# A decoder layer on one core: where the gate product y, the sums of x and attention's setup stand

## The chip, the cores and the metric

The kernel runs on one core of a Trainium2 chip. A core has five engines with a queue of instructions each: TensorE (PE in the profile; PEld is its weight load), VectorE (DVE), ScalarE (ACT), GpSimd (POOL) and SyncE (SP), which here only starts transfers. They wait for one another by semaphores. The metric is the time of one execution in microseconds, from the device; less is better.

## What is computed

One decoder layer over 16 sequences of 256 tokens with 256 features, each part followed by a residual sum and a LayerNorm:

```python
def _L0_attn_ref(x, ...):                    # the mixer
    xh, gate = split(x @ W_in.T + b_in)
    xh = silu(causal_conv(xh, conv_w) + conv_b)
    s  = scan of (xh @ W_ssm.T + b_ssm)      # one number for each token
    y  = (s * xh + Dv * xh) * silu(gate)
    return y @ W_out.T + b_out + x
def _L0_xattn_ref(query, key, value, ...):   # 16 heads of 16, key = value = ctx
    return softmax(q @ k.T / 4) @ v @ Wo.T + bo
def _L0_ffn_ref(x, Wr, W1, W2):              # router, 8 experts of capacity 640
    ...
x = _layernorm(x + _L0_attn_ref(x, ...))
x = _layernorm(x + _L0_xattn_ref(x, ctx, ctx, ...))
x = _layernorm(x + _L0_ffn_ref(x, ...))
```

## The kernel before

Three functions run one after the other, each a block with one program for each engine. `mixer_in` (to about 143 us) makes `gated`, the product of `xh` and silu of the gate, for all tokens, and the scan's result, which four transfers write to HBM. `attend` (to about 680 us) does the rest of the mixer, the cross attention and the router, and sends the rows to their experts. `experts` does the experts and the last LayerNorm.

`attend` is a software pipeline over the 16 sequences, here called batches. A step `n` has 16 slots `h`, and every engine's program walks the same slots, doing for each what its list says. In step n, batch n+1 is in its first stage (lag −1: `y`, output projection of the mixer, residual `r`, LayerNorm), batch n makes k and q, batch n−1 takes row maxima of the scores, batches n−2 and n−3 the exponentials and weighted sums, and batch n−4 the router and the scatter. A step from 6 to 13 is run by a loop of two; the others are written out. What the order is in a queue is what is written: an engine never passes a waiting instruction. TensorE alone loads weights ahead.

The places that matter here, by line:

- L1032, VectorE, slot 7: `y = (sb + d_col) * gated` in four chunks of 128 × 256, one semaphore count `y_done` after the fourth. Both tensors are in SBUF. `sb` is the scan's row, broadcast by a transfer (L521).
- L707, TensorE, slots 11 and 13: `mixer_out`, the product of `y` with the output weights, two halves of tokens; each sums over the four chunks. The first half waits for `y_done`.
- L984, VectorE, and L744, TensorE, even slots: the scores of two heads go to PSUM and VectorE takes their row maxima `nmax`. TensorE's scores of the next even slot wait for the maxima of this one, since there is one buffer.
- L615 and L617, GpSimd, `residual`: `x2b = x + b_out`, then `x2b + x`, both 128 × 512. VectorE's `r` (L1062, slot 13) adds `x2b` to the product and waits for `x_added`.
- L621, GpSimd, `split_lo`: the low half of k, and of q, for a product in two halves. Its input is ScalarE's cast (L876). SyncE then writes both to HBM and reads them back in another layout.
- L650, GpSimd: two indirect transfers that scatter a batch's rows to their experts; they wait for `dest` (L1048, VectorE, slot 10).
- L1039 to L1056, VectorE, slots 8 to 11: `place`, `carry`, `over`, `slot`, and `onrm`, which TensorE waits for.
- L602 to L606, L949 to L958: attention's setup. GpSimd fills 32 rows in each half of `kst` with ones, of which row 48 of each half is used (the others are overwritten by keys or unused). VectorE scales the weights and bias of q (`w_q_sb`, `bq`) and casts `tri` and `ones`.

GpSimd's order in a step is what this quotes (L621, L615, L650 are the calls' contents):

```python
if on(n, 0): split_lo(n, s["k_hi"], s["k_split"])
if on(n, 4): ...                     # norm of batch n - 4, L633 to L639
if on(n, 0) and on(n, -1): residual(n + 1, q)
if on(n, 0): split_lo(n, s["q_hi"], s["q_split"])
if on(n, 4): ...                     # the scatter, L645 to L653
```

## Time and profile before

| | us |
|---|---|
| median of 3 runs | 957.1 (956.09 to 959.01) |
| the profiled execution | 958.14 |
| its span, first to last instruction | 956.4 |
| mean granted TensorE clock | 0.927 |
| busy: PE, PEld, DVE, ACT, POOL | 802.6, 638.8, 611.7, 401.8, 357.6 |

The profile covers one execution. A busy time is the time in which an engine has an instruction in work; the share of a whole span mixes stages with different limits. The releaser of a wait is inferred from semaphores: it names what came last. Rows of a timeline merge instructions that follow one another, so that the duration is that from the first one's start to the last one's end.

### The profile page before, as it was taken

Reading aid. Unit: us, or ns where it says so; the run is one execution under the profiler, and the core shown is the slowest. Engines: PE = TensorE matmul, PEld = TensorE weight load, DVE = VectorE, ACT = ScalarE, POOL = GpSimd, SP = SyncE. Lnnn points to the kernel's source line nnn. Section 1 sums busy time; section 2 is a strip of 40 time slices with the busy share of each in tenths; the row PEclk is TensorE's granted clock in tenths of the full one; section 3 lists DMA queues with packets and bytes.
Section 4 is the critical chain, followed back from the end, with each engine's and each line's share of the span. In section 5 each row is a group of like instructions: output and inputs, shape, how many; then the busy total and the mean of one; then the engine's idle time right before and its main releaser. Section 6 shows DMA issues by size and latency. Waiting matters only on the chain. (4 is left out here: it accounts for less than half of the span.)

```text
span 956.4 us, 16891 instructions
## 1 busy us (share of the span) xinstructions
PE 802.6 (84%) x5933; PEld 638.8 (67%) x5933; DVE 611.7 (64%) x1410; ACT 401.8 (42%) x639; POOL 357.6 (37%) x290
## 2 busy tenths in 40 slices
PE   5999864678988889988889898874599999999992
PEld 3777653455766666666666675542499999999982
DVE  4888847365787887787887877533245555545542
ACT  4665631135544545444555456540334233423320
POOL 0333326322345454344544343233122254325422
PEclk9999887689999999999999999885599999999997
DMA  4115501645435534435434434102432333234000
GB/s 123 45 46 168 169 2 53 156 138 139 135 120 151 149 116 114 148 118 158 124 116 135 133 114 143 45 31 85 131 102 74 117 126 100 76 115 140 22 27 18
DMA packets 75913, 100.91 MB, mean 106 GB/s; under 512 B 10961, under 2 KB 63354, under 8 KB 75856
## 3 DMA queue, kind: packets, MB, share of 16 engines
q1 hardware_dynamic: 72400, 92.03, 32.3%
q0 software_dynamic: 3456, 8.13, 2.4%
q8 instruction: 34, 0.56, 0.2%
q14 instruction: 23, 0.19, 0.1%
HBM read 65.47 MB, written 35.74 MB: 106 GB/s over the span
## 5 line engine op out<-in xcount | busy, mean ns | idle before, releaser
L984 DVE TENSOR_REDUCE nmax<-ps_m 128x4 f32<-128x1024 f32 x128 | 156.4, 1222 | 56.4 <-PE ps_m L744 49.2
L938 ACT ACTIVATE pt<-ps_a 128x1024 f32<-128x1024 f32 x128 | 131.3, 1026 | 120.2 <-PE ps_a L754 87.4
L1249 ACT ACTIVATE hid<-ps_h 128x640 fp32r<-128x640 f32 x64 | 45.1, 705 | 152.1 <-PE ps_h L1189 152.1
L1189 PE MATMUL ps_h<-xt,w_hi 128*128 128x320 f32 x512 | 100.7, 319 | 1.0 <-DVE xt L1264 1.0
L744 PE MATMUL ps_m<-kst,qst 48*128 48x256 f32 x512 | 67.6, 344 | 34.1 <-DVE nmax L984 28.7
L1298 DVE SCALAR_TENSOR_TENSOR hid<-ps_h,hid 128x640 fp32r<-128x640 f32 x64 | 52.8, 825 | 57.0 <-ACT hid L1249 56.5
L744 PEld LDWEIGHTS ps_m<-kst,qst 48*128 48x128 f32 x512 | 40.5, 195 | 72.0 <-DVE nmax L984 47.5
L1201 PE MATMUL ps_y<-w_hi,hid 128*128 128x256 f32 x640 | 85.3, 284 | 1.7 <-issue 1.7
L1189 PEld LDWEIGHTS ps_h<-xt,w_hi 128*128 128x128 f32 x512 | 80.6, 192 | 5.5 <-DVE hid L1298 3.6
L1201 PEld LDWEIGHTS ps_y<-w_hi,hid 128*128 128x128 f32 x640 | 80.1, 191 | 1.9 <-issue 1.9
L707 PE MATMUL ps_d<-w_out_sb,y 128*128 128x256 f32 x256 | 67.3, 412 | 11.2 <-DVE y L1032 10.9
L166 POOL TENSOR_TENSOR gated<-xh,sgate 128x512 f32<-128x512 f32 x32 | 42.3, 1321 | 90.1 <-ACT xh L259 90.1
L354 DVE SCALAR_TENSOR_TENSOR conv<-ps_xh,taps,conv 128x510 f32<-128x510 f32 (+2 forms) x96 | 71.7, 747 | 3.4
L769 PE MATMUL ps_o<-pt,vals 128*32 128x256 f32 x1024 | 71.3, 398 | 0.0
L1345 POOL DMA_INDIRECT out_rows<-gated,token x40 | 39.4, 986 | 84.1 <-issue 84.1
L621 POOL TENSOR_TENSOR half<-kq,half 128x512 fp32r<-128x512 f32 x32 | 42.7, 1335 | 71.8 <-ACT half L876 71.8
L650 POOL DMA_INDIRECT rows_dram<-pay,dest x32 | 33.1, 1035 | 86.0 <-DVE dest L1048 76.0
L707 PEld LDWEIGHTS ps_d<-w_out_sb,y 128*128 128x128 f32 x256 | 50.3, 206 | 19.8 <-issue 11.5
L1312 DVE SCALAR_TENSOR_TENSOR gated<-ps_y,gated 128x256 f32<-128x256 f32 x40 | 19.3, 483 | 64.8 <-PE ps_y L1201 61.6
L1189 PE MATMUL ps_h<-xt,w_lo 128*128 128x320 f32 x256 | 59.1, 312 | 0.0
L1333 POOL TENSOR_TENSOR w_lo<-gated,w_hi 128x2048 fp32r<-128x2048 f32 x8 | 47.4, 5919 | 28.0 <-ACT w_hi L1239 27.9
L754 PE MATMUL ps_a<-qst,kst 49*128 49x256 f32 x512 | 53.9, 289 | 0.8 <-ACT pt L938 0.5
(169 smaller groups left out, 1623.8 us busy)
## 6 DMA issues: line engine op xcount, KB each, us to landing
halves_dram<-half SPq DMA_DIRECT2D x64, 256.0 KB, 2.6
gated<-in_w SPq DMA_DIRECT2D x16, 1024.0 KB, 5.2
kst<-halves_dram SPq DMA_DIRECT2D x64, 128.0 KB, 2.6
qst<-halves_dram SPq DMA_DIRECT2D x64, 128.0 KB, 2.9
rows_dram<-blank SPq DMA_DIRECT2D x1, 5160.0 KB, 19.4
gated<-rows_dram SPq DMA_DIRECT2D x8, 645.0 KB, 4.2
x_raw<-in_x_t SPq DMA_DIRECT2D x8, 512.0 KB, 3.8
xres<-in_x SPq DMA_DIRECT2D x16, 256.0 KB, 4.1
```

The source lines that it names most:

```text
L354: op = nc.vector.scalar_tensor_tensor(out[:, :, late:S], ps[:, :, 0:S - late], taps[:, m, k:k + 1], out[:, :, late:S], ALU.mult, ALU.add)
L707: mm = pe.matmul(ps_d[:, t * D:(t + 1) * D], y[:, m, t * P:(t + 1) * P], w["out"][:, m, :], start=(m == 0), stop=(m == MH - 1), skip_group ...
L744: mm = pe.matmul(ps_m[:, side, t, :], qst[base:base + MR, p, k, t * P:(t + 1) * P], kst[base:base + MR, p, k, :], start=True, stop=True, s ...
L754: mm = pe.matmul(ps_a[:, side, t, :], kst[base:base + MR + 1, p, k, t * P:(t + 1) * P], qst[base:base + MR + 1, p, k, :], start=True, stop ...
L769: mm = pe.matmul(ps_o[VW * i:VW * (i + 1), g, :], vals[:, p, t, h, :], pt[:, h // 2 % 4, h % 2, t, :], start=(t == 0), stop=(t == KT - 1), ...
L938: nc.scalar.activation(pt[:, k % 4].rearrange("p s t q -> p (s t q)"), ps_a[:].rearrange("p s t q -> p (s t q)"), ACT.Exp).then_inc(s["exp ...
L984: nc.vector.tensor_reduce(nmax[:, q, :, :, h // 2].rearrange("p t s -> p s t"), ps_m[:], AX.X, ALU.max, negate=True).then_inc(s["max_done" ...
L1189: mm = pe.matmul(ps_h[:, f % 2, c2, 0:HC], w1[a][:, p, k, f * P:(f + 1) * P], xt[:, b, p, k, c2 * HC:(c2 + 1) * HC], start=(n == 0 and k = ...
L1201: mm = pe.matmul(ps_y[:, (p + t) % 2, 0:D], hid[:, a, f, t * P:(t + 1) * P], w2[b][:, p, f, :], start=(n == 0 and f == 0), stop=(n == 2 an ...
L1249: nc.scalar.activation(hid[:, HI, f, :].rearrange("p (c n) -> p c n", c=2), ps_h[:, f % 2, :, 0:HC], ACT.Relu).then_inc(s["hid_hi"], 1)
L1298: nc.vector.scalar_tensor_tensor(hid[:, LO, f, :].rearrange("p (c n) -> p c n", c=2), ps_h[:, f % 2, :, 0:HC], 0.0, hid[:, HI, f, :].rearr ...
L1333: nc.gpsimd.tensor_tensor(flat(w2[LO][:, p]), flat(w2_raw), flat(w2[HI][:, p]).bitcast(F32), ALU.subtract).then_inc(s["w2_lo"], 1)
```

## The change

`y` goes from slot 7 to slot 9 on VectorE, behind the maxima of slot 8 and the first `onrm`, and counts `y_done` after each of the four chunks; the first half of `mixer_out` waits chunk by chunk. On GpSimd the sums of x go behind the subtraction for q and behind the scatter. The scaled weights and bias and the casts are made by ScalarE at the end of `mixer_in`'s program, in tiles that outlive it. The memsets of `kst` are gone: ScalarE copies the ones into a tile of 32 × 128, and SyncE copies that by two transfers into the one row of `kst` per half that is read. The waits on the setup change with it.

```diff
@@ mixer_in, ScalarE @@
             xh_of(MH * NG - 1)
             inject_out(NG - 1)
+            act.wait_ge(c["loaded"], 16 * len(c["loads"]))
+            nc.scalar.mul(c["w"]["q"][:], c["w"]["q"][:], HD ** -0.5).then_inc(c["scaled"], 1)
+            nc.scalar.mul(c["bq"][:], c["b_q"][:], HD ** -0.5).then_inc(c["scaled"], 1)
+            nc.scalar.copy(c["tri_b"][:], c["tri"][:]).then_inc(c["scaled"], 1)
+            nc.scalar.copy(c["ones_b"][:], c["ones"][:]).then_inc(c["scaled"], 1)
+            nc.scalar.copy(c["ones_r"][:], c["ones"][0:NH * S // P, :]).then_inc(c["scaled"], 1)
@@ attend, SyncE @@
-                need(sp, s["y_done"], j - 1)
+                need(sp, s["y_done"], MH * (j - 1))
...
-                sp.wait_ge(s["setup_pool"], 3)
+                settled(sp)
...
+            for base in SIDES:
+                sp.dma_start(kst[base + MR:base + MR + 1, :, :, :].rearrange("o b k t -> o (b k t)").bitcast(F32),
+                             c["ones_r"][:].bitcast(F32)).then_inc(s["ones_in"], 16)
             sp.wait_ge(c["scan_out"], 64)
@@ attend, GpSimd @@
-            for base in SIDES:
-                nc.gpsimd.memset(kst[base + 2 * HD:base + 4 * HD, :, :, :].bitcast(F32), 1.0).then_inc(s["setup_pool"], 1)
-            pool.wait_ge(s["setup_pool"], 3)
...
-                if on(n, 0) and on(n, -1):
-                    residual(n + 1, q)
                 if on(n, 0):
                     split_lo(n, s["q_hi"], s["q_split"])
...
                         ).then_inc(sent[p], 16)
+                if on(n, 0) and on(n, -1):
+                    residual(n + 1, q)
@@ attend, TensorE @@
-            pe.wait_ge(s["setup_dve"], 6)
-            pe.wait_ge(s["setup_pool"], 3)
+            pe.wait_ge(s["setup_dve"], 2)
+            pe.wait_ge(c["scaled"], 5)
+            pe.wait_ge(s["ones_in"], 32)
...
-                    pe.wait_ge(s["y_done"], j + 1)
...
                 for m in range(MH):
+                    if t == 0:
+                        pe.wait_ge(s["y_done"], MH * j + m + 1)
@@ attend, VectorE @@
-            nc.vector.tensor_scalar(w["q"][:], w["q"][:], SCALE, None, ALU.mult).then_inc(s["setup_dve"], 1)
-            nc.vector.tensor_scalar(bq[:], c["b_q"][:], SCALE, None, ALU.mult).then_inc(s["setup_dve"], 1)
-            nc.vector.tensor_copy(tri[:], c["tri"][:]).then_inc(s["setup_dve"], 1)
-            nc.vector.tensor_copy(ones_b[:], ones[:]).then_inc(s["setup_dve"], 1)
...
-                    if h == 7 and on(n, -1):
+                    if h == 9 and on(n, -1):
                         dve.wait_ge(s_in[q], use(n + 1, 16, q))
                         need(dve, s["wout_mm"], n + 1)
                         for m in range(MH):
-                            op = nc.vector.scalar_tensor_tensor(y[:, m, :], sb[:, q], c["d_col"][:, m:m + 1],
-                                                                gated[:, m, bass.ds((n + 1) * S, S)], ALU.add, ALU.mult)
-                        op.then_inc(s["y_done"], 1)
+                            nc.vector.scalar_tensor_tensor(y[:, m, :], sb[:, q], c["d_col"][:, m:m + 1],
+                                                           gated[:, m, bass.ds((n + 1) * S, S)], ALU.add, ALU.mult
+                                                           ).then_inc(s["y_done"], 1)
```

VectorE in the loop of `attend`, slots 7 to 10, before (`L984` are the maxima, `L1032` is `y`, `L1048` is `dest`):

```order
L1027 TENSOR_TENSOR carry<-carry,hot 128x8
...
L1032 SCALAR_TENSOR_TENSOR y<-sb,d_col_sb,gated 128x256
...
L984 TENSOR_REDUCE nmax<-ps_m 128x2x2
L1037 TENSOR_REDUCE place<-sel 128x2
L1039 TENSOR_TENSOR carry<-carry,hot 128x8
L1042 TENSOR_SCALAR over<-place 128x2
...
L1056 TENSOR_TENSOR onrm<-ps_e,rec 128x256
...
L984 TENSOR_REDUCE nmax<-ps_m 128x2x2
L1048 TENSOR_TENSOR dest<-slot,over 128x2
```

And with the change:

```order
L1027 TENSOR_TENSOR carry<-carry,hot 128x8
...
L984 TENSOR_REDUCE nmax<-ps_m 128x2x2
L1030 TENSOR_REDUCE place<-sel 128x2
L1032 TENSOR_TENSOR carry<-carry,hot 128x8
L1035 TENSOR_SCALAR over<-place 128x2
...
L1049 TENSOR_TENSOR onrm<-ps_e,rec 128x256
...
L1056 SCALAR_TENSOR_TENSOR y<-sb,d_col_sb,gated 128x256
...
L984 TENSOR_REDUCE nmax<-ps_m 128x2x2
L1041 TENSOR_TENSOR dest<-slot,over 128x2
```

The four instructions of `y` moved over one pair of maxima and six small operations, and stand directly ahead of the maxima of slot 10 and `dest`.

GpSimd in the same loop, before:

```order
L637 TENSOR_SCALAR twice<-pay,mv,ve 128x256 x2
...
L615 TENSOR_TENSOR x2b<-xres,b_out_sb 128x512
...
L617 TENSOR_TENSOR x2b<-x2b,xres 128x512
L621 TENSOR_TENSOR half<-kq,half 128x512
L650 DMA rows_dram<-pay,dest 5120x258 x2
L656 TENSOR_TENSOR ve<-ve,power 128x2
```

And with the change:

```order
L639 TENSOR_SCALAR twice<-pay,mv,ve 128x256 x2
L623 TENSOR_TENSOR half<-kq,half 128x512
L650 DMA rows_dram<-pay,dest 5120x258 x2
...
L617 TENSOR_TENSOR x2b<-xres,b_out_sb 128x512
...
L619 TENSOR_TENSOR x2b<-x2b,xres 128x512
L658 TENSOR_TENSOR ve<-ve,power 128x2
```

The two sums moved from ahead of the subtraction for q to behind the scatter's two transfers, which wait for `dest`.

## Rows read from the trace of the kernel before

**Rows 1.** Busy time by stretch: PE, PEld, DVE, ACT, POOL, granted clock, DMA share, GB/s
```profile
363.00:393.00 30.00, 26.53 (x213) 19.01 (x213) 23.12 (x57) 14.73 (x26) 13.27 (x12) 0.94 0.45 130
393.00:421.00 28.00, 24.87 (x213) 17.92 (x213) 23.17 (x57) 14.75 (x26) 13.28 (x12) 1.00 0.40 123
```
**Rows 2.** Timeline, batch 10 in step 9: start, duration, engine, line, operation, idle before
```profile
407.86 0.51 PE L744 MATMUL ps_m<-kst,qst 48*128 48x256 f32 x4 [0.48 <-DVE nmax L984]
...
408.61 0.61 ACT L876 CAST half<-kq 128x512 fp32r<-128x512 f32 x1
408.74 3.70 DVE L1032 SCALAR_TENSOR_TENSOR y<-sb,d_col_sb,gated 128x256 f32<-128x256 f32 x4
408.87 1.48 POOL L617 TENSOR_TENSOR x2b<-x2b,xres 128x512 f32<-128x512 f32 x1
...
410.31 1.45 POOL L621 TENSOR_TENSOR half<-kq,half 128x512 fp32r<-128x512 f32 x1
...
412.36 1.22 DVE L984 TENSOR_REDUCE nmax<-ps_m 128x4 f32<-128x1024 f32 x1
...
413.63 0.50 PE L744 MATMUL ps_m<-kst,qst 48*128 48x256 f32 x4 [1.71 <-DVE nmax L984]
...
414.18 0.42 DVE L1056 TENSOR_TENSOR onrm<-ps_e,rec 128x256 f32<-128x256 f32 x1
...
415.65 0.15 DVE L1048 TENSOR_TENSOR dest<-slot,over 128x2 int32<-128x2 f32 x1
...
416.66 1.09 POOL L650 DMA_INDIRECT rows_dram<-pay,dest  x1 [4.90 <-DVE dest L1048]
...
418.07 0.97 POOL L650 DMA_INDIRECT rows_dram<-pay,dest  x1 [0.31 <-issue]
...
421.07 0.69 DVE L1062 TENSOR_TENSOR r<-ps_d,x2b 128x512 f32<-128x512 f32 x1 [2.32 <-PE ps_d L707]
```
**Rows 3.** Timeline, step 15, which has no `y` and no sums of x
```profile
581.31 1.30 POOL L621 TENSOR_TENSOR half<-kq,half 128x512 fp32r<-128x512 f32 x1 [2.04 <-ACT half L876]
...
581.44 1.20 DVE L1042 TENSOR_SCALAR over<-place 128x2 f32<-128x2 f32 x1
```
**Rows 4.** Timeline, attention's start, and the landing times of the loads of `sb`
```profile
143.30 7.23 POOL L606 MEMSET kst<- 32x4096 f32 x2
...
144.86 0.36 SPq L521 DMA_DIRECT2D sb<-scan_dram  x1
...
150.61 1.26 POOL L615 TENSOR_TENSOR x2b<-xres,b_out_sb 128x512 f32<-128x512 f32 x1
...
151.22 3.13 DVE L1032 SCALAR_TENSOR_TENSOR y<-sb,d_col_sb,gated 128x256 f32<-128x256 f32 x4 [0.20 <-DVE b_o_sb L958]
...
154.50 5.08 PE L707 MATMUL ps_d<-w_out_sb,y 128*128 128x256 f32 x16 [9.72 <-DVE y L1032]
...
162.51 0.84 ACT L867 ACTIVATE kq<-ps_d,b_k_sb 128x256 f32<-128x256 f32 x2 [27.93 <-PE ps_d L687]
...
DMA to landing us min/median/max: 3.0/3.7/4.1
```
**Rows 5.** Timeline, step 1, in which batch 2 has its `y`
```profile
191.70 1.23 DVE L984 TENSOR_REDUCE nmax<-ps_m 128x4 f32<-128x1024 f32 x1 [1.56 <-PE ps_m L744]
...
192.61 1.27 POOL L621 TENSOR_TENSOR half<-kq,half 128x512 fp32r<-128x512 f32 x1 [4.84 <-ACT half L876]
...
196.54 0.50 PE L744 MATMUL ps_m<-kst,qst 48*128 48x256 f32 x4
...
201.60 2.03 PE L687 MATMUL ps_d<-ctx,w_k_sb 128*128 128x256 f32 x4 [2.19 <-DMA ctx<-in_ctx_t]
```
**Rows 6.** Timeline, step 14, in which batch 15 has its `y`
```profile
554.22 1.66 DVE L1032 SCALAR_TENSOR_TENSOR y<-sb,d_col_sb,gated 128x256 f32<-128x256 f32 x4
...
559.49 0.15 DVE L1048 TENSOR_TENSOR dest<-slot,over 128x2 int32<-128x2 f32 x1
...
564.88 0.69 DVE L1062 TENSOR_TENSOR r<-ps_d,x2b 128x512 f32<-128x512 f32 x1 [2.32 <-PE ps_d L707]
```

More of the change, by code:

```diff
@@ L400, in attend @@
     gated = c["gated"]
-    w, eye, ones = c["w"], c["eye"], c["ones"]
+    w, eye, bq, tri, ones_b = c["w"], c["eye"], c["bq"], c["tri_b"], c["ones_b"]
     KT = S // P
@@ L410, in attend @@
     NG4 = NH // PV
-    SCALE = HD ** -0.5
     xres = T("xres", [P, KT, D], F32)
@@ L441, in attend @@
     hot, carry = T("hot", [P, KT, E], BF16), T("carry", [P, E], BF16)
-    tri, ones_b = T("tri", [P, P], BF16), T("ones_b", [P, P], BF16)
     sel, place = T("sel", [P, KT, E], F32), T("place", [P, KT], F32)
@@ L445, in attend @@
     dest = T("dest", [P, 2, KT], I32)
-    bq = T("bq", [P, KD], F32)
     ps_m = PS("ps_m", [P, 2, KT, S], F32)
@@ L453, in attend @@
     hscr = c["hscr"]
-    names = """setup_pool setup_dve setup_pe vo_row x_in0 x_in1 ctx_in0 ctx_in1 x_added
+    names = """setup_pool setup_dve setup_pe ones_in vo_row x_in0 x_in1 ctx_in0 ctx_in1 x_added
         s_in0 s_in1 k_mm v_mm wout_mm x1t_mm q_mm mt_mm y_done k_out q_out k_hi q_hi k_split q_split v_out r1_done var1_ready
@@ L592, in _ @@
             run(sp, step)
-            sp.wait_ge(s["y_done"], B)
+            sp.wait_ge(s["y_done"], MH * B)
             sp.dma_start(c["w1_raw"], dram["w1"][0:D, :].rearrange("(k p) f -> p k f", p=P)).then_inc(c["w1_in"], 16)
@@ L906, in step @@
                         if isinstance(n, int) and n == 0:
-                            act.wait_ge(s["setup_dve"], 6)
+                            act.wait_ge(c["scaled"], 5)
                         add_bias(bq, s["q_out"])
@@ L951, in _ @@
             dve.wait_ge(c["loaded"], 16 * len(c["loads"]))
-            nc.vector.tensor_scalar(w["q"][:], w["q"][:], SCALE, None, ALU.mult).then_inc(s["setup_dve"], 1)
-            nc.vector.tensor_scalar(bq[:], c["b_q"][:], SCALE, None, ALU.mult).then_inc(s["setup_dve"], 1)
-            nc.vector.tensor_copy(tri[:], c["tri"][:]).then_inc(s["setup_dve"], 1)
-            nc.vector.tensor_copy(ones_b[:], ones[:]).then_inc(s["setup_dve"], 1)
             dve.wait_ge(s["setup_pe"], 1)
             nc.vector.tensor_tensor(c["b_o"][:], c["b_o"][:], ps_d[:, 0:D], ALU.add).then_inc(s["vo_row"], 1)
-            dve.wait_ge(s["setup_dve"], 6)
-            dve.wait_ge(s["setup_pool"], 3)
+            dve.wait_ge(s["setup_dve"], 2)
+            dve.wait_ge(c["scaled"], 5)
             dve.wait_ge(s["vo_row"], 1)
@@ L1027, in step @@
                         nc.vector.tensor_tensor(carry[:], carry[:], hot[:, 0, :], ALU.add).then_inc(s["place_done"], 1)
-                    if h == 7 and on(n, -1):
-                        dve.wait_ge(s_in[q], use(n + 1, 16, q))
-                        need(dve, s["wout_mm"], n + 1)
-                        for m in range(MH):
-                            op = nc.vector.scalar_tensor_tensor(y[:, m, :], sb[:, q], c["d_col"][:, m:m + 1],
-                                                                gated[:, m, bass.ds((n + 1) * S, S)], ALU.add, ALU.mult)
-                        op.then_inc(s["y_done"], 1)
                     if h == 8 and on(n, 4):
@@ L1058, in step @@
                                                 ).then_inc(s["on_done"], 1)
+                    if h == 9 and on(n, -1):
+                        dve.wait_ge(s_in[q], use(n + 1, 16, q))
+                        need(dve, s["wout_mm"], n + 1)
+                        for m in range(MH):
+                            nc.vector.scalar_tensor_tensor(y[:, m, :], sb[:, q], c["d_col"][:, m:m + 1],
+                                                           gated[:, m, bass.ds((n + 1) * S, S)], ALU.add, ALU.mult
+                                                           ).then_inc(s["y_done"], 1)
                     if h == 13 and on(n, -1):
@@ L1399, in decoder @@
                 c[n] = load(n, [P, width])
-            for n in ("loaded", "blank_ready", "rows_blank", "scan_out"):
+            for n, shape, dt in (("bq", [P, KD], F32), ("tri_b", [P, P], BF16), ("ones_b", [P, P], BF16),
+                                 ("ones_r", [NH * S // P, P], F32R)):
+                c[n] = hold(n, shape, dt)
+            for n in ("loaded", "blank_ready", "rows_blank", "scan_out", "scaled"):
                 c[n] = sem(n)
```

## The prediction, made before the result was known

> **What bounds the kernel now.** I read four views in this order: the busy time of the engines in cut stretches, the timeline of one batch in attention's steady part, the timeline of the last batch, and the timeline of attention's start. The stretches [rows 1] are cut from one start of `r` to the next: a batch takes 30.0 or 28.0 us, TensorE is busy 26.5 or 24.9 of it and VectorE 23.1 or 23.2. No engine is full, so the time of a batch is a chain between TensorE and VectorE, and a microsecond is worth something only where both wait for it. The difference of 2.0 us goes with the granted clock, 0.94 against 1.00.
>
> In the steady batch [rows 2] the reader should see one wait: VectorE is at `y` from 408.74 to 412.44, the maxima of slot 8 follow at 412.36, although their scores were written at 408.37 (407.86 + 0.51), and TensorE waits 1.71 us for them, until 413.63. `y` takes 3.70 us for four instructions; the same four take 1.66 where GpSimd is idle [rows 6]. Beside the long one stand GpSimd's two additions and one subtraction, each also longer (1.48, 1.45) than alone (1.27 in [rows 5]): the two engines take turns, and each turn of GpSimd costs VectorE its length. At the end of the batch VectorE waits 2.32 us for TensorE's product of `y` before `r` at 421.07. So the delay by `y` travels slot 8 maxima, slot 10 scores, both products of `y`, `r`, and from there into the next batch.
>
> **The change, part by part.**
>
> *Ten steady batches (y of batches 5 to 14).* I follow [rows 2] with the new order. GpSimd no longer has the sums of x ahead of the subtraction for q. That subtraction's input is ready at 409.22 (408.61 + 0.61, ScalarE's cast), so it runs about 409.3 to 410.6 instead of 410.31 to 411.76. The maxima of slot 8 start at 408.4 and end at 409.6. The small VectorE operations behind them meet the subtraction: in the last batch, which has no `y`, the operation `over` took 1.20 us beside it and ended with it (582.64 against 582.61) [rows 3]. So they are through at 410.6. From there to the end of `onrm` the old trace needs 0.9 us (413.58, end of the maxima, to 414.60, less the first two small ones); that gives 411.5. `y` then runs alone, 1.66 us, to 413.2. Maxima of slot 10: 1.22, to 414.4, and `dest` is done at 414.4 instead of 415.80. TensorE meanwhile does not wait for slot 8: its scores of slot 10 and its first product come up to 2.0 us earlier (1.71 and the 0.3 it waited for `onrm`), and this is where the semaphore per chunk pays, since that product would start at about 413.1 when `y` has one chunk left.
>
> The sums of x now stand behind the scatter. Old rows: the scatter's first transfer starts 0.86 after `dest` (415.80 to 416.66), both take 2.38 (to 419.04). Then the sums, 1.26 for the first [rows 4] and about 1.3 for the second with 0.07 between: 2.65. All together 5.9 us behind `dest`, which is 420.3, and `r` at 420.35. TensorE's product would have allowed 419.0. So of a possible 2.0 us only 421.07 − 420.35 = **0.72 us** is left, and what `r` now waits for is GpSimd. From `r` on nothing changes: VectorE works through the next slots without a hole, and the later start is passed on. Ten batches: **−7.2**. Both ends: the product sets `r`, −2.05 each, −20.5; or `dest` comes no earlier than before, then `r` is at 415.80 + 5.9 = 421.74, +0.67 each, +6.7. I take the worked value because every duration in it has a row.
>
> *Batches 2, 3 and 4, before the scatter has begun.* There the sums follow the subtraction directly, and `y` is now behind the maxima of slot 8. In the first of them [rows 5] the maxima end at 192.93; the subtraction holds GpSimd's turn until 193.88; then `y` and the two sums alternate, 1.66 + 1.28 + 1.3, to 198.1. The maxima of slot 10 (1.2) come to 199.3, and the scores of slot 12 follow at 199.35, not at 196.54. That is 2.8 us, and the old order had put `y` into a hole. Against it: the products of k waited 2.19 us for their transfer (201.60) anyway. Lower end 0 (if `y` keeps its turn for all four, 195.6, maxima to 196.8), upper end 2.8; I take 1.5, the middle, for each of three: **+4.5** (0 to 8.4).
>
> *Batch 15.* Its `y` was not stretched (1.66) [rows 6], so there is nothing to win, and `dest` at 559.64 plus 5.9 gives `r` at 565.55 instead of 564.88: **+0.7** (0 to 1.1).
>
> *Batch 1.* Its `y` meets no maxima on VectorE before or after. Its sums move behind the subtraction for q, so its `r` is later by two turns of GpSimd at most (2.6); the cover is the wait of the next products of k for the context's transfer, which is 2.19 us even one batch later [rows 5]. I take 0, and without that cover it costs up to 2.6.
>
> *Attention's start.* Gone are two memsets of 32 × 4096 on GpSimd, 7.23 us to 150.53, and VectorE's four setup operations; only then come the first sum of x (150.61) and `y` (151.22) [rows 4]. The load of `sb` is issued at 144.86, and nearby loads of this tile land after 3.0 to 4.1 us, so it is there at about 148.9, and x, next in the queue, at about 149.3. `y` now starts at 148.9 instead of 151.22, and its last chunk, alternating with the sums as before (3.13, or 4.2 with both sums inside), ends at about 153.1 instead of 154.35. TensorE took 5.08 us for its 16 products after all of `y`; with chunks only two of the first eight and the second eight are left after 153.1: 10/16 of 5.08 is 3.2, to 156.3 instead of 159.58, 3.3 earlier, and `r` with it. If TensorE's clock stays at 2.4 GHz there, 1.6 and not 3.2 us, 4.9 earlier. If `y` and the sums never meet, 5.3. I take **−3.8**, near the end with the old duration, range 3.2 to 5.3.
>
> The setup itself costs nothing where it went. ScalarE's five instructions are one of 128 × 512 (a cast of that size takes 0.61) and four smaller ones, under 3 us; ScalarE's first work of attention, at 162.51, had waited 27.93 us [rows 4]. If that cover were gone they would cost these 3 us. The row of ones adds two transfer issues to SyncE's queue, about 0.9 us by the neighbours (0.36 for the load at 144.86 [rows 4]), ahead of a wait of that queue for the scan's result; they land before `y`. Cover gone: 0.9 us later for the first loads.
>
> **Sum:** −3.8 − 7.2 + 4.5 + 0.7 = −5.8. The profiled execution took 958.14 us (span 956.4 and 1.7 around it) and would take 952.3; it is 1.0 above the median of the three runs, 957.1, for which I say **951.3 us**.
>
> **Where a page speaks otherwise.** The rows show the granted clock at 0.94 in the batch of 30.0 us and 1.00 in that of 28.0, that is, one stretch at 1.2 GHz costs about 2 us. The Trainium skill, page "TensorE: Matmul & The Clock Gate", part 1, says that the low clock is the default and that activity of the engine releases it, while idleness brings it back. By this rule, which the two rows fit, a kernel whose TensorE has one hole less may lose fewer stretches; it is the rival "clock" below.
>
> **Rivals.**
> 1. *The sums behind the scatter are the new bound (slower).* `r` waits for x: break-even is `dest` done at 421.07 − 5.9 = 415.13 in the frame of [rows 2]. If one more turn of GpSimd falls into the small operations or into `y` (1.0 to 1.3 us each), `dest` is at 415.7 and the ten batches cost +6.7 in place of −7.2: −3.8 + 6.7 + 4.5 + 0.7 = +8.1, 965.2 us. For it: the whole margin is 0.7 us, and the subtraction now lies right in front. Against: by its input it must end at 410.6, 0.9 before `y`. 0.16.
> 2. *The product stays the bound.* If GpSimd is done in time, each batch wins 2.05: −3.8 − 20.5 + 4.5 + 0.7, 938 us. It would need the sums to be over at 419.0, right when the scatter alone ends at 417.7. 0.08.
> 3. *It cancels.* The three early batches cost 2.8 each, the steady ones win 0.3: −3.3 − 3 + 8.4 + 1.1 = +3.2, and with 0.7 won it is −1. Between 954.3 and 960. Speaks for it: in both places the gain hangs on tenths. 0.20.
> 4. *Clock.* From `r` at 421.07 to `r` at 564.88 [rows 2, 6] five batches take 143.8 us, 3.8 more than five of 28.0, which is two stretches of 2.0; so about four in the ten. Without them the forecast is 8 lower, 943. 0.13. That more are added is in the range above.
>
> **Numbers.** The forecast's case (946 to 954) has 0.43. Faster by over 0.3% (below 954.2; 0.3% is about what a measurement of this kernel tells from no change): 0.43 + 0.08 + 0.13 = 0.64; within: 0.20; slower: 0.16. The range 942 to 962 leaves out rival 2 and the upper half of rival 1.
>
> **What would show it.** In the changed profile: `y` at 1.7 us in steady batches, the 1.71 us wait before slot 10's scores gone, VectorE's wait before `r` ended by `x2b` of GpSimd and not by the product, `r` to `r` 27.3 us at full clock. In batches 2 to 4 `y` at about 4.2 us and `r` to `r` longer than before. The first `r` at about 155 to 156. Wrong it would be if `r` is still released by TensorE (rival 2), if `r` to `r` is above 28.0 (rival 1), or if the sum comes from batches at another granted clock (rival 4).

## The result and the profile after

| | before | after |
|---|---|---|
| median, us | 957.0 (956.09 to 959.01, 4 runs) | 942.4 (940.32 to 944.36, 4 runs) |
| ratio to before, 95% interval | | 0.984 (0.982 to 0.987) |
| the profiled execution, us | 958.14 | 941.63 |
| its span, us | 956.4 | 939.8 |
| mean granted clock | 0.927 | 0.933 |

The kernel became 14.6 us faster. The forecast was 951.3, a gain of 5.7; 942.4 lies at the lower edge of its range. The stretches between the starts of `r` show where the gain came from. A granted clock of 1.00 is TensorE's full clock here, and a low-clock stretch is a time in which the granted clock was 0.50, 1.2 of 2.4 GHz. Busy time by stretch of the kernel after, in the columns of [rows 1]: first two steady batches at full clock, then the ten batches from `r` of batch 4 to `r` of batch 14.

```profile
383.44:410.66 27.22, 24.83 (x212) 17.95 (x211) 21.11 (x58) 14.73 (x27) 12.98 (x12) 1.00 0.47 142
410.66:438.16 27.50, 24.89 (x212) 18.01 (x212) 21.07 (x57) 14.83 (x27) 13.00 (x12) 1.00 0.48 139
...
245.59:520.07 274.48, 251.27 (x2121) 181.43 (x2122) 210.29 (x570) 148.23 (x261) 130.06 (x120) 0.99 0.46 139
```

The same ten batches of the kernel before:

```profile
249.17:537.07 287.90, 255.71 (x2112) 184.03 (x2112) 231.31 (x570) 147.15 (x260) 132.81 (x120) 0.98 0.45 132
```

They took 13.4 us less. Before, these ten have four stretches of 3.4 us at the lower clock, and the four batches that hold them take 30.0 us in place of 28.0; after, they have one, which costs 0.9 us. So the 13.4 us fall into two parts of about equal size: ten times 28.0 against ten times 27.35 at full clock, 6.5 us, and the cost of the low-clock stretches, 8 us before and 0.9 after, 7 us. One stretch of the kernel before, with the granted clock in the column before the last two:

```profile
386.00:389.40 3.40, 3.40 (x15) 2.39 (x13) 0.75 (x5) 0.00 (x0) 2.06 (x2) 0.50 0.76 227
```

The whole, span against span:

| part | before | after | difference | forecast |
|---|---|---|---|---|
| start to attention's first instruction | 143.1 | 140.2 | −2.9 | 0 |
| from there to the first `r` | 16.5 | 12.5 | −4.0 | −3.8 |
| `r` of batch 0 to `r` of batch 4 | 89.6 | 92.9 | +3.3 | +4.5 |
| `r` of batch 4 to `r` of batch 14 | 287.9 | 274.5 | −13.4 | −7.2 |
| `r` of batch 14 to `r` of batch 15 | 27.8 | 27.3 | −0.5 | +0.7 |
| `r` of batch 15 to the end | 391.5 | 392.4 | +0.9 | 0 |

The first line is no effect of the change: of its instructions only ScalarE's five stand ahead of that point, behind ScalarE's last work of the mixer. Over the twelve runs below attention starts anywhere from 140.2 to 143.5 us, and it goes with the clock that the mixer was granted in that execution: where 6.8 us of the mixer were at the low clock (the kernel after, three of those with the new setup, and y_twice with the old one) it starts at 140.2 to 140.6, where 10.2 us were, at 141.8 to 143.5, and where 13.7 us were (before, hole_filled), at 143.1 and 143.2.

Timeline of the kernel after, batch 10 in step 9, to be laid beside [rows 2] (start, duration, engine, line, operation, idle before and what ended it); its batch begins at the `r` of 383.44, that of [rows 2] at 393.0:

```profile
398.87 1.23 DVE L984 TENSOR_REDUCE nmax<-ps_m 128x4 f32<-128x1024 f32 x1 [0.45 <-PE ps_m L748]
...
399.78 1.27 POOL L623 TENSOR_TENSOR half<-kq,half 128x512 fp32r<-128x512 f32 x1 [1.76 <-ACT half L880]
...
400.09 0.98 DVE L1032 TENSOR_TENSOR carry<-carry,hot 128x8 bf16<-128x8 bf16 x1
...
401.81 1.66 DVE L1056 SCALAR_TENSOR_TENSOR y<-sb,d_col_sb,gated 128x256 f32<-128x256 f32 x4
402.32 0.50 PE L748 MATMUL ps_m<-kst,qst 48*128 48x256 f32 x4
...
403.48 1.89 PE L711 MATMUL ps_d<-w_out_sb,y 128*128 128x256 f32 x8
...
404.53 0.15 DVE L1041 TENSOR_TENSOR dest<-slot,over 128x2 int32<-128x2 f32 x1
...
405.54 1.09 POOL L650 DMA_INDIRECT rows_dram<-pay,dest  x1 [4.49 <-DVE dest L1041]
...
407.92 1.28 POOL L617 TENSOR_TENSOR x2b<-xres,b_out_sb 128x512 f32<-128x512 f32 x1
...
409.28 1.27 POOL L619 TENSOR_TENSOR x2b<-x2b,xres 128x512 f32<-128x512 f32 x1
...
410.66 0.69 DVE L1062 TENSOR_TENSOR r<-ps_d,x2b 128x512 f32<-128x512 f32 x1 [3.58 <-POOL x2b L619]
```

`y` takes 1.66 us, not 3.70. TensorE's scores at 402.32 have no wait where those of [rows 2] had 1.71. A wait of 0.9 to 1.5 us for the maxima now stands elsewhere, about 3.3 us behind `r`, in nine of the ten batches. `dest` is through 21.2 us after the batch's `r` (404.68 − 383.44), against 22.8 before. And `r` waits 3.58 us for GpSimd's `x2b`, no longer for the product. From `dest` to `r` it is 5.98 us; the forecast had 5.9.

Attention's start in the kernel after, beside [rows 4], and step 1 and batch 1's `r`, beside [rows 5]:

```profile
131.43 0.62 ACT L293 ACTIVATE w_q_sb<-w_q_sb 128x512 f32<-128x512 f32 x1
...
140.23 1.26 SPq L558 DMA_DIRECT2D kst<-ones_r  x2
...
145.62 3.70 DVE L1056 SCALAR_TENSOR_TENSOR y<-sb,d_col_sb,gated 128x256 f32<-128x256 f32 x4 [3.37 <-DMA sb<-scan_dram]
146.25 2.93 PE L711 MATMUL ps_d<-w_out_sb,y 128*128 128x256 f32 x6 [4.53 <-DVE y L1056]
...
152.68 0.69 DVE L1062 TENSOR_TENSOR r<-ps_d,x2b 128x512 f32<-128x512 f32 x1 [3.36 <-PE ps_d L711]
...
167.03 0.69 DVE L1062 TENSOR_TENSOR r<-ps_d,x2b 128x512 f32<-128x512 f32 x1 [7.14 <-POOL x2b L619]
...
185.39 4.46 DVE L1056 SCALAR_TENSOR_TENSOR y<-sb,d_col_sb,gated 128x256 f32<-128x256 f32 x4
186.31 1.45 POOL L617 TENSOR_TENSOR x2b<-xres,b_out_sb 128x512 f32<-128x512 f32 x1
```

ScalarE's setup lies in its idle time, and the two transfers of ones take SyncE's queue 1.26 us. `y` now waits for the transfer of `sb`, and TensorE begins 0.63 us after it. In batch 1, `r` waits 7.14 us for the sums, and in batch 2 `y`, both sums and the end of the subtraction take turns, 4.46 us.

### The profile page after: what moved, and what is told of

Its sections match the earlier page's. It is cut to its first block and busy times, and to the rows that moved or that the text cites. A ratio compares the mean times of both kernels' runs of the same rounds, so it can differ in the third digit from the quotient of the medians.

```text
span 939.8 us, 16918 instructions
## 1 busy us (share of the span) xinstructions
PE 798.8 (85%) x5933; PEld 634.7 (68%) x5933; DVE 589.4 (63%) x1406; ACT 403.4 (43%) x644; POOL 347.7 (37%) x288
## 5 line engine op out<-in xcount | busy, mean ns | idle before, releaser
L984 DVE TENSOR_REDUCE nmax<-ps_m 128x4 f32<-128x1024 f32 x128 | 156.6, 1223 | 46.6 <-PE ps_m L748 39.5
L711 PE MATMUL ps_d<-w_out_sb,y 128*128 128x256 f32 x256 | 63.8, 393 | 5.8 <-DVE y L1056 4.9
L711 PEld LDWEIGHTS ps_d<-w_out_sb,y 128*128 128x128 f32 x256 | 47.2, 196 | 15.4 <-issue 5.6
L1333 POOL TENSOR_TENSOR w_lo<-gated,w_hi 128x2048 fp32r<-128x2048 f32 x8 | 47.3, 5907 | 27.9 <-ACT w_hi L1239 27.8
```

Source lines behind the costliest of these rows:

```text
L711: mm = pe.matmul(ps_d[:, t * D:(t + 1) * D], y[:, m, t * P:(t + 1) * P], w["out"][:, m, :], start=(m == 0), stop=(m == MH - 1), skip_group ...
L984: nc.vector.tensor_reduce(nmax[:, q, :, :, h // 2].rearrange("p t s -> p s t"), ps_m[:], AX.X, ALU.max, negate=True).then_inc(s["max_done" ...
L1333: nc.gpsimd.tensor_tensor(flat(w2[LO][:, p]), flat(w2_raw), flat(w2[HI][:, p]).bitcast(F32), ALU.subtract).then_inc(s["w2_lo"], 1)
```

## The experiments

Ratios are to the kernel before on the same chip, with the 95% interval. The columns in the middle come from each kernel's trace: the time from attention's first instruction to the first `r`, from `r` of batch 0 to that of batch 4, from 4 to 14, and how many low-clock stretches begin in those ten batches. The ratios come from 5 to 12 executions of each kernel, the other columns from one trace each.

| kernel | ratio | start to r0 | r0 to r4 | r4 to r14 | low-clock stretches |
|---|---|---|---|---|---|
| before (first profile) | 1 | 16.5 | 89.6 | 287.9 | 4 |
| setup_only | 0.997 (0.994 to 0.999) | 15.5 | 90.3 | 291.0 | 6 |
| order_only | 0.987 (0.984 to 0.990) | 15.8 | 93.6 | 274.3 | 1 |
| y_only | 0.972 (0.968 to 0.976) | 15.8 | 88.1 | 260.3 | 0 |
| sums_only | 0.977 (0.973 to 0.981) | 16.7 | 89.4 | 268.7 | 0 |
| hole_filled | 0.998 (0.995 to 1.000) | 16.5 | 92.5 | 281.3 | 0 |
| hole_full | 1.002 (0.999 to 1.005) | 16.6 | 93.5 | 281.4 | 0 |
| hole_steady | 0.992 (0.989 to 0.995) | 16.7 | 89.4 | 284.5 | 2 |
| y_twice | 1.005 (1.003 to 1.006) | 19.1 | 90.3 | 289.7 | 4 |
| after_sums_ahead | **0.963 (0.960 to 0.965)** | 12.5 | 89.5 | 260.5 | 0 |
| no_chunks | 0.987 (0.984 to 0.989) | 15.6 | 98.7 | 272.9 | 0 |
| chunkless_ahead | 0.976 (0.974 to 0.979) | 15.5 | 91.0 | 268.8 | 0 |
| after_again | 0.982 (0.980 to 0.985) | 12.5 | 93.5 | 274.2 | 1 |

### The change taken apart

**setup_only** is the kernel after with `y` back in slot 7, the count per batch and the sums ahead of the subtraction; what is left of the change is the setup by ScalarE and the row of ones by transfers.

> The kernel before with the setup's part alone (ScalarE's five instructions, the ones by transfers, no memsets); y in slot 7, sums ahead. Both theories: the first r stands 15.4 us after attention's first instruction with one y_done per batch (16.5 before, 12.6 with the whole change) or down to 12.6 if the chunks do nothing there; from the first r on nothing differs. Time 953 to 956 by that. Clock theory: steady batches 28.0 us each where the granted clock is 1.00 and 30.0 where it is not, and some of both, since the wait of 1.71 us is still there. Rival (the stretches of low clock have nothing to do with that wait): the number of 30 us batches may be anything.

0.997: faster, by 3.2 us of 964.4, the median of before on this chip. Yet its `r` comes 15.5 us after attention's start, only 1.0 us earlier than before. `y` is through 2.1 us earlier after attention's start, but the sixteen products behind it then lie almost wholly at the low clock and take 6.13 us in place of 5.08 [rows 4]. The forecast's 3.8 us for attention's start need the chunks as well.

**order_only** is the reverse: the kernel before with the two moves and no new setup.

> The kernel before with y in slot 9 by chunks and the sums behind the scatter; old setup. Worked schedule alone: ten steady batches at 27.35 in place of 28.0 (-6.5), batches 1 to 4 +3.4, so -3: 954. Clock theory: the wait of 1.71 us is gone, so the four stretches of low clock in steady batches go too, -8 more: 946, with at most one batch above 28. Rival: 954 and batches above 29 remain.

0.987, and r to r 27.2 and 27.5 by turns. One low-clock stretch in ten batches, as in the kernel after. The two moves together carry the larger part of the gain.

**y_only** moves `y` alone to slot 9, by chunks, and leaves the sums ahead:

```diff
-                    if h == 7 and on(n, -1):
...
+                    if h == 9 and on(n, -1):
```

> The kernel before with y in slot 9 by chunks; the sums of x stay ahead of the subtraction, old setup. If what limits the changed kernel's steady batch is that r waits for the sums behind the scatter, then here r waits for the product of y again and the batch is 26.4 us (28.0 less 1.6) at full clock, against 27.35: ten batches -16, early batches about +1, so 941; with the clock theory's -8, 933. Rival (the sums had to move, since ahead of the subtraction they hold it and the maxima back): 27.5 us or more a batch, 948 and over.

0.972, twice the gain of both moves together. `y` takes 1.66 us in nine of the ten steady batches (2.12 in batch 6) and `r` is released by the product again. The timeline of one steady batch of y_only:

```profile
376.25 0.69 DVE L1063 TENSOR_TENSOR r<-ps_d,x2b 128x512 f32<-128x512 f32 x1 [2.32 <-PE ps_d L708]
...
393.35 1.26 POOL L621 TENSOR_TENSOR half<-kq,half 128x512 fp32r<-128x512 f32 x1
...
395.24 1.66 DVE L1057 SCALAR_TENSOR_TENSOR y<-sb,d_col_sb,gated 128x256 f32<-128x256 f32 x4
...
402.18 0.69 DVE L1063 TENSOR_TENSOR r<-ps_d,x2b 128x512 f32<-128x512 f32 x1 [2.32 <-PE ps_d L708]
```

25.93 us from `r` to `r`: that is the 26.0 which the forecast gave the product alone (419.0 − 393.0). In slot 9 `y` comes when GpSimd is through with all three operations, even with the sums ahead.

**sums_only** moves the sums alone behind the scatter:

```diff
-                if on(n, 0) and on(n, -1):
-                    residual(n + 1, q)
                 if on(n, 0):
                     split_lo(n, s["q_hi"], s["q_split"])
...
+                if on(n, 0) and on(n, -1):
+                    residual(n + 1, q)
```

> The kernel before with the sums of x behind the scatter and y still in slot 7. y there meets only the subtraction for q: 2.9 us in place of 3.7. dest 0.7 us earlier, the sums over 5.9 behind it, so r at the same place as before: steady batch 27.9 to 28.0, batch 1 +2.3. Time 957 to 959; by the clock theory with a wait of 1.0 instead of 1.7 us still some batches at 30. Rival (moving the sums is itself the gain): below 952.

My number, 957 to 959 us, was missed; the rival held. The timeline of one steady batch of sums_only:

```profile
383.43 0.69 DVE L1062 TENSOR_TENSOR r<-ps_d,x2b 128x512 f32<-128x512 f32 x1 [3.10 <-POOL x2b L617]
...
398.29 1.67 DVE L1032 SCALAR_TENSOR_TENSOR y<-sb,d_col_sb,gated 128x256 f32<-128x256 f32 x4
...
399.73 1.36 POOL L621 TENSOR_TENSOR half<-kq,half 128x512 fp32r<-128x512 f32 x1 [1.76 <-ACT half L876]
...
403.95 0.15 DVE L1048 TENSOR_TENSOR dest<-slot,over 128x2 int32<-128x2 f32 x1
...
410.10 0.69 DVE L1062 TENSOR_TENSOR r<-ps_d,x2b 128x512 f32<-128x512 f32 x1 [3.08 <-POOL x2b L617]
```

`y` in slot 7 starts before GpSimd has anything to do, and the subtraction waits for it, not the other way round. `dest` is through 20.7 us after `r` (404.10 − 383.43) and `r` follows 6.0 behind it, 26.67. With `y` in slot 9 it stands ahead of `dest`, which is then through after 21.2 us. That is why both moves together (27.2 to 27.5) are slower than either alone (25.9 to 26.3 and 26.7 to 27.0). Either move alone removes the collision in the steady batches; the second then adds only its own cost.

### The clock

Among these kernels the low-clock stretches go with the wait of 1.7 us ahead of slot 10's scores: four and six of them where it is (before, setup_only), one or none where it is not. In before and setup_only each of these ten stretches begins 0.6 to 2.1 us after the end of that wait; but six batches of before and four of setup_only have the same wait and no stretch. Four runs change that wait, and with it the time that TensorE is idle in a batch, while the rest of the order stays.

**hole_filled** and **hole_full** are the kernel before with the second half of the values' product made two times (the diff, shortened) and three. They repeat work whose result is the same, in the wait, here called the hole:

```diff
-                for k in range(KD):
-                    mm = pe.matmul(ps_d[...], ctx[...], w["v"][:, k, :], ...)
+                for _ in range(2 if t == KT - 1 else 1):
+                    for k in range(KD):
+                        mm = pe.matmul(ps_d[...], ctx[...], w["v"][:, k, :], ...)
```

> The kernel before, with the second half of the products for the values (four weight loads and four products, 0.94 us) made twice; the repeat lands in the wait of 1.71 us that TensorE has ahead of slot 10's scores, so that about 0.8 us of it is left. Clock theory (the low-clock stretches of the steady batches come from that hole): the five or six stretches of 3.4 us in the steady part go away or become fewer, r to r is 28.0 in nearly every batch, and the whole is up to 8 us shorter than before, ratio 0.990 to 0.997, although TensorE does more work. Rival (the stretches belong to y's alternation with GpSimd or to chance): r to r stays a mix of 28.0 and 30.0, ratio 1.000 to 1.003. If 0.8 us left is still enough of a hole, this run looks like the rival and hole_full decides.

> As hole_filled, but the second half of the values is made three times (1.88 us more on TensorE, against a wait of 1.71), so the hole ahead of slot 10's scores is gone and slot 10 is about 0.2 us late. Clock theory: no low-clock stretch in the steady batches, r to r about 28.1, ratio 0.990 to 0.998. Rival (not the hole): mix of 28.2 and 30.2, ratio 1.002 to 1.005.

The wait ahead of slot 10's scores is about 0.85 us in hole_filled and gone in hole_full; `y` still takes 3.70 us in both. Neither has a low-clock stretch in the ten batches, which take 281.3 and 281.4 us, 6.5 less than before. One steady batch of hole_filled:

```profile
408.45 3.70 DVE L1033 SCALAR_TENSOR_TENSOR y<-sb,d_col_sb,gated 128x256 f32<-128x256 f32 x4
...
409.74 2.76 PE L697 MATMUL ps_d<-w_v_sb,ctx 128*128 128x256 f32 x12
...
413.34 0.50 PE L745 MATMUL ps_m<-kst,qst 48*128 48x256 f32 x4 [0.85 <-DVE nmax L985]
```

So the steady batches went as the clock theory said, but the whole did not: 0.998 (0.995 to 1.000) is just above the range expected for hole_filled, and 1.002 (0.999 to 1.005) is what the rival had given hole_full. In the profiles the four early batches, which have no such hole of 1.7 us, are longer by 2.9 and 3.9 us, and the part behind the last `r`, which the edit does not touch, by 2.9 and 5.6. **hole_steady** therefore repeats only in the loop (`if t == KT - 1 and not isinstance(j, int)`), steps 6 to 13:

> As hole_filled, but the repeat (0.94 us of TensorE) is made only in the eight steps that are written as a loop (steps 6 to 13); the early batches, where hole_filled lost 2.9 us because TensorE is the bound there, are those of the kernel before. Clock theory: no low-clock stretch between r of batch 7 and r of batch 14, r to r 28.0 to 28.4 there, the eight steps about 5 us shorter than with four stretches, ratio 0.992 to 0.996: more work in less time. Rival (hole_filled's clean clock was chance): mix of 28.0 and 30.0, ratio 1.000 or above.

0.992 (0.989 to 0.995): TensorE does more and the kernel is 7 us faster (951.9 against 959.0). The eight batches of the loop, before and in hole_steady (columns of [rows 1]):

```profile
304.99:537.07 232.08, 205.97 (x1690) 148.04 (x1690) 185.15 (x456) 117.87 (x208) 106.18 (x96) 0.97 0.45 132
```

```profile
307.23:532.76 225.53, 206.32 (x1722) 149.89 (x1723) 185.11 (x457) 117.86 (x208) 106.22 (x96) 1.00 0.45 134
```

Clock 0.97 against 1.00, 32 products more, 6.55 us less. Its two stretches lie ahead of the loop, in batches of 29.4 and 29.5 us whose code is that of before; there the first profile of before has none. So where the hole is, the number of stretches varies from one execution to the next.

**y_twice** goes the other way. It is sums_only, without stretches and without the hole, with the four instructions of `y` run first into a spare tile:

```diff
+                        for m in range(MH):
+                            op = nc.vector.scalar_tensor_tensor(spare[:, m, :], ...)
...
                         for m in range(MH):
                             op = nc.vector.scalar_tensor_tensor(y[:, m, :], ...)
```

> The kernel sums_only (sums of x behind the scatter, y in slot 7, r to r 26.6 to 27.0, no low-clock stretch in the steady part), with the four instructions of y run a second time into a spare tile just ahead of it: VectorE has 1.66 us more work there, and nothing of GpSimd's is beside it. It puts the hole of TensorE before slot 8's maxima back without the alternation of the two engines. Clock theory: r to r 28.2 to 28.5 at full clock (1.66 more each) and low-clock stretches of about 3.4 us return in several steady batches, 30.2 there; whole 0.977 + 25/960 + up to 8/960 = 1.003 to 1.012. Rival (the alternation makes the stretches): r to r 28.2 to 28.5 in every batch, 0.998 to 1.003.

1.005. One steady batch:

```profile
411.03 2.68 DVE L1038 SCALAR_TENSOR_TENSOR y<-sb,d_col_sb,gated 128x256 f32<-128x256 f32 x4
...
414.91 0.50 PE L745 MATMUL ps_m<-kst,qst 48*128 48x256 f32 x4 [1.42 <-DVE nmax L985]
```

With a hole of 1.42 us four stretches are back in the ten batches, at 271, 370, 445 and 503 us, three of them 1.2 to 1.4 us behind the hole and the one at 370 elsewhere; batches are 28.4 to 28.8 us, those with a stretch 29.2 to 29.9. One thing was not as I wrote: the subtraction of GpSimd falls beside the second `y`, which takes 2.68 us, so some alternation is back too. The two filled kernels speak against this as the cause, since they keep the whole alternation and lose the stretches.

The hole is not the only wait that comes before a stretch. The kernel after, order_only and after_again have one stretch each, and each begins 0.8 to 1.2 us after the end of the new wait behind `r`, here in after_again (the stretch begins at 332.1):

```profile
330.87 0.50 PE L748 MATMUL ps_m<-kst,qst 48*128 48x256 f32 x4 [1.46 <-DVE nmax L984]
```

Eight other batches of each have that wait too, 0.7 to 1.5 us of it, and no stretch. One rival to the single hole was not tried. All these edits also change how long TensorE is idle in a batch in all: 3.0 to 3.5 us in before and setup_only and 2.6 to 3.9 in y_twice, but 2.2 to 2.6 in hole_filled, 2.1 to 2.7 in nine of the ten batches of the kernel after, and at most 2.9 in the others. Whether the one wait counts, its place or the sum of the waits, these runs do not separate.

### The best combination, and the price of the chunks

**after_sums_ahead** is the kernel after with the sums put back ahead of the subtraction (the diff of sums_only, reversed).

> The changed kernel with the sums of x put back ahead of the subtraction for q: the setup by ScalarE and y in slot 9 by chunks stay. Theory (the sums behind the scatter are what r waits for in the changed kernel, the change of y's place is the whole gain of the order, the setup's gain of 3.8 us at attention's start adds to it): steady r to r 25.9 to 26.3 with r released by TensorE's product, as in y_only, first r 12.6 to 15.4 us after attention's start; ratio 0.972 - 0.004 = 0.968 (0.964 to 0.973), faster than both the kernel before and the changed one (0.984). Rival (the setup's gain is swallowed with the sums ahead, as it nearly was in setup_only, 0.997): 0.970 to 0.974.

0.963 (0.960 to 0.965), 924.0 us against 958.9 of before on that chip; the changed kernel has 0.982 to 0.984. The start (12.5 us) and the steady batches (25.8 to 26.3) are each as good as in the best part. In its steady batches:

```profile
394.59 1.66 DVE L1056 SCALAR_TENSOR_TENSOR y<-sb,d_col_sb,gated 128x256 f32<-128x256 f32 x4
395.60 1.89 PE L711 MATMUL ps_d<-w_out_sb,y 128*128 128x256 f32 x8
...
401.53 0.69 DVE L1062 TENSOR_TENSOR r<-ps_d,x2b 128x512 f32<-128x512 f32 x1 [2.32 <-PE ps_d L711]
```

The product starts 1.01 us into `y`, ahead of its last chunks. **no_chunks** and **chunkless_ahead** are the kernel after and after_sums_ahead with one count per batch (the diff, shortened):

```diff
                         for m in range(MH):
-                            nc.vector.scalar_tensor_tensor(y[:, m, :], ...).then_inc(s["y_done"], 1)
+                            op = nc.vector.scalar_tensor_tensor(y[:, m, :], ...)
+                        op.then_inc(s["y_done"], 1)
```

> The changed kernel with one count of y_done per batch again (TensorE's first product of y waits for all four chunks); everything else as in the changed kernel. Theory (in the steady batches r waits for the sums of x behind the scatter, 3.6 us of idle time, so a product that starts later is hidden; at attention's start r waits for the product): steady r to r 27.2 to 27.5 as before, first r about 15.4 us after attention's start in place of 12.5, whole 2 to 3 us above the changed kernel, ratio 0.986 to 0.989. Rival (my prediction's: the chunks pay in the steady batch): 27.8 or more per batch, ratio 0.992 or more.

> The kernel after_sums_ahead (0.9625; r released by TensorE's product, r to r 25.9 to 26.3) without the chunks: one count of y_done per batch. Here nothing of GpSimd's hides a later product: if TensorE waits for the last chunk of y, each batch is 0.3 to 1.2 us longer (26.3 to 27.3), and with 2.9 at attention's start the whole is 6 to 15 us above after_sums_ahead, 0.969 to 0.978. Rival (TensorE reaches the product only when y is complete anyway): only the start is later, 0.965 to 0.967.

no_chunks has 0.987, and its steady batches are 27.2 to 27.5 us, those of the kernel after. Two things are behind this. TensorE comes to the product only when `y` is through, with chunks (403.48, `y` ends at 403.47) as without:

```profile
409.38 1.66 DVE L1055 SCALAR_TENSOR_TENSOR y<-sb,d_col_sb,gated 128x256 f32<-128x256 f32 x4
...
411.09 1.99 PE L710 MATMUL ps_d<-w_out_sb,y 128*128 128x256 f32 x8
```

And `r` waits 3.3 to 3.5 us for the sums, which would hide a product that came later. What the chunks win there is 3.1 us at attention's start (15.6 against 12.5) and, in this profile, some 5 us in the four early batches (98.7 against 93.5 and 92.9), of which the medians, 946.7 against 942.0 for after_again, show less. In chunkless_ahead, where the product is what `r` waits for, the same edit costs 0.83 us a batch (268.8 against 260.5), and the whole rises from 0.963 to 0.976:

```profile
401.53 1.66 DVE L1055 SCALAR_TENSOR_TENSOR y<-sb,d_col_sb,gated 128x256 f32<-128x256 f32 x4
...
403.25 1.99 PE L710 MATMUL ps_d<-w_out_sb,y 128*128 128x256 f32 x8 [0.54 <-DVE y L1055]
```

**after_again** is the kernel after itself, for the spread of its clock.

> The changed kernel itself, beside the others on one chip: 0.984 (0.981 to 0.988), steady r to r 27.2 to 27.5 and at most one low-clock stretch from r of batch 4 to r of batch 14. If the missing stretches of the first profile had been chance, there are four or more here and r to r has batches of 29 and more.

0.982 (0.980 to 0.985), one stretch in the ten batches, 274.2 us. So two profiles of this kernel have one stretch each, where one of before has four.

## Why the prediction was right and where it failed

**The step that failed** is rival 4, "Clock": it was left out of the sum and given 0.13. It said that "about four in the ten" stretches cost 2.0 us each and that the forecast would be "8 lower, 943" without them. There were four, and the kernel lost three of them and about half of the cost of the last, 7 us. I treated the stretches as something beside the change, though the change takes away the wait of 1.71 us that these stretches follow. hole_steady shows it without the change: with that wait halved, eight batches take 6.55 us less. y_twice, with a wait of 1.42 us, has four stretches again. The forecast's last sentence named this as what would make it wrong ("if the sum comes from batches at another granted clock"), and that is what the profile shows. The rule of the Trainium skill that was quoted there, page "TensorE: Matmul & The Clock Gate", part 1 (activity releases the low clock, idleness brings it back), agrees with these runs.

That the result is as near to 943 as it is owes something to chance. Span against span the kernel is 10.8 us better than the forecast's sum. The ten batches give 6.2 of that (about 7 from the clock, less 0.7 by which the schedule's part fell short), the mixer 2.9, which is no effect of the change, the early batches and batch 15 1.2 each, the start 0.2, and the end takes 0.9 back.

**Ten steady batches, −7.2.** The schedule's part was right in place and nearly in size. Forecast were `y` at 1.66, the wait of 1.71 gone, `dest` after 21.4 us (414.4 − 393.0), `r` released by `x2b`, 27.35 from `r` to `r`. Measured: 1.66, no wait, 21.2, `x2b`, and 27.2 and 27.5 by turns. At full clock that is −0.65 a batch in place of −0.72. Only one detail was elsewhere: beside the subtraction it is `carry` that is stretched (0.98 us), where [rows 3] had `over`.

**"This is where the semaphore per chunk pays"** was wrong for the steady batch. no_chunks has the same batch. The forecast put the product at 413.1 with one chunk of `y` left, 20.1 us behind the batch's `r`; it began 20.04 us behind it, and there `y` was through. An earlier product would have gained nothing either, which is what the forecast's own 419.0 against 420.35 says.

**Attention's start, −3.8.** Measured −4.0, in both profiles of the kernel after. The text had it from two causes, and the runs show that neither is worth that alone: −1.0 with the new setup, −0.7 with the chunks (y_only), −4.0 with both. The clock has a part in this, which the forecast named and left out: in before, setup_only and y_only a stretch of 13.7 us at the low clock reaches into the products of `y`, in the kernel after and after_sums_ahead this stretch lasts 10.2 us. How much of the −4.0 that is was not measured. `sb` landed within 3.8 us of its issue (141.81 to 145.62), in the range of [rows 4].

**Batches 2 to 4, +4.5, and batch 1, 0.** Together +3.3 was measured, so the sum is near, and the mechanism for batches 2 and 3 is as described: `y` and both sums by turns, 4.46 us where 4.2 was forecast (batch 4 has 3.70). The granted clock differs here too: 30.7 us of this part are at the low clock in the kernel after and 23.9 in before; setup_only, with 34.1, takes 90.3 us, so that most of the +3.3 is not the clock. But the first part of the reason does not hold. In y_only `y` stands behind the maxima as well, and the four batches take 88.1 us, not longer than before; the sums behind the subtraction without the later `y` cost nothing either (sums_only, 89.4). It needs both. In batch 1, which had 0 with up to 2.6 uncovered, `r` waits 7.14 us for the sums, and that interval is 2.3 us longer; the transfer of the context did not cover it, though the next interval returned 0.9.

**Batch 15, +0.7.** It was −0.5. The kernel before has a low-clock stretch there (at 549.8 us) and the kernel after has none; against setup_only, which has the old order and no stretch there, 28.0 us, it is −0.7 (though its `y` took 3.70 us there and that of before 1.66). So the sign of the term was wrong, for a size too small to matter.

**Rival 1** did not come: no turn of GpSimd falls into `y`. **Rival 2** gave the product 26.0 us; it does bound the kernel so, but only if the sums stay where they were. What nothing in the forecast considered is that one of the two moves would be better alone.

Open is the time from the last `r` to the end, 390.2 to 400.1 us, with code that none of the edits touches. Four of the five kernels above 395.8, with VectorE busy for 199 to 205 us in that part and not 195, are the first four, which ran on one chip, whose median of before was 964.4 and not 957.0 to 959.0. Whether it is the chip was not tried. The fifth, hole_full with 397.1 us, ran on another chip and has VectorE busy for 195 us; its cause is open. So each ratio should be read beside the stretches of the trace.

## What to carry to other kernels

When work of two engines collides, moving one of the two may be enough. Here either move ended the collision, and both together put the second behind something else (0.987 with both, 0.977 and 0.972 with one). Try each move alone before both. And when batches differ by a whole low-clock stretch, look at which wait of TensorE comes before the stretches: here the wait of 1.7 us cost another 0.8 us a batch in clock (8 us over ten batches), and an edit that removed it won both.

## What the runs showed of the hardware

That useless products can shorten a kernel: in hole_steady 32 more products in eight batches gave 6.55 us back, because the granted clock went from 0.97 to 1.00 (of the two levels, 1.2 and 2.4 GHz, only the higher is left in those batches). With a wait of 1.71 us ahead of slot 10's scores there were four and six stretches in the ten batches (before, setup_only), with one of 1.42 four, with one of 0.85 in its place none. With a wait of 0.9 to 1.5 us at another place of the batch, in the kernel after, there was one; so the length of one wait does not decide alone, and what else enters these runs don't tell.

What a stretch costs: in the ten batches of before each lasts 3.4 us and its batch is 2.0 longer. In the others of these traces it is 0.9 (the kernel after) to 1.9 us, by where the stretch falls. In the kernel before it lies over the product of `y`, whose eight instructions take 3.12 us in place of 1.89:

```profile
383.96 0.50 PE L744 MATMUL ps_m<-kst,qst 48*128 48x256 f32 x4 [1.71 <-DVE nmax L984]
...
385.48 3.12 PE L707 MATMUL ps_d<-w_out_sb,y 128*128 128x256 f32 x8
```

That the turns of VectorE and GpSimd depend on what VectorE reads. The maxima, which read PSUM, took 1.22 or 1.23 us with a GpSimd operation beside them or without; `y`, which reads two tiles in SBUF, took 1.66 or 3.70. The Trainium skill, page "SBUF — State Buffer", section "Who interferes with whom", describes the pair of ports that the two engines share as a lock held for the whole instruction, which a VectorE operation with two SBUF inputs needs and a GpSimd operation that reads SBUF too; the rows agree. Which of the two comes first decides here: in sums_only `y` comes first, keeps its 1.67 us, and the subtraction takes 1.36.
